# Distance attention: the square root as a power on GpSimd, the clip as a rectified sum on ScalarE; the shared expert in two places

## The reference

```python
scores = jax.nn.sigmoid(xf @ gate_w + bias)
top_scores, top_idx = jax.lax.top_k(scores, K)
top_scores = top_scores / (jnp.sum(top_scores, axis=-1, keepdims=True) + 1e-06)
...
combined = jnp.einsum('teh,te->th', eo * 0.1, w)
shared = (jax.nn.gelu(xf @ sw_up + sb_up, approximate=False) @ sw_down + sb_down) * 0.1
out = (shared + combined).reshape(b, s, h)
out = out / (jnp.max(jnp.abs(out), axis=-1, keepdims=True) + 1e-06)
```

```python
p = jax.nn.softmax(s_, axis=-1) * maskb.astype(scores.dtype)
cum = jnp.cumsum(p, axis=-1)
tot = jnp.sum(p, axis=-1, keepdims=True)
...
dist_scores = jnp.sqrt(jnp.clip((tot - cum) * pos, 0.0, None))
gamma = -jax.nn.softplus(gammas)[None]
diff = jnp.exp(jax.nn.sigmoid(pdiff))[:, None]
total_effect = jnp.clip(jnp.exp(dist_scores * gamma * diff), 1e-05, 100000.0)
scores = scores * total_effect
scores = jax.nn.softmax(scores, axis=-1)
```

## Time and profile before

| | us |
|---|---|
| median of 2 runs | 3798.94 (3797.53 to 3800.35) |
| profiled execution | 3777.61 |
| its span | 3775.8 |

### The profile page before, as it was taken

The page is one execution under the profiler, slowest core; times in us unless marked ns, Lnnn a source line. Parts: engine busy times, 40 slices in busy tenths (PEclk is TensorE's granted clock), DMA queues, the critical chain, the costliest instruction groups (busy, mean ns, idle before and its releaser), DMA issues. The chain is left out here.

```text
span 3775.8 us, 52084 instructions
## 1 busy us (share of the span) xinstructions
PE 3035.1 (80%) x15676; PEld 1663.4 (44%) x15676; DVE 2050.2 (54%) x5067; ACT 1638.2 (43%) x2348; POOL 901.5 (24%) x1035
## 2 busy tenths in 40 slices
PE   5899759687899999875669978899556777777777
PEld 3333459423344444562332245799532434333443
DVE  6677511595333333350478841011367888888853
ACT  1466311120233333220127742233136998898963
POOL 2000010351000000000010003000335777777750
PEclk8899879899999999888879988999877999999998
DMA  4111246341333243349422131599541000000002
GB/s 144 43 47 47 74 163 255 126 167 62 89 71 98 63 105 79 105 181 426 179 72 60 56 125 45 213 345 345 194 146 20 15 17 22 17 22 17 23 9 59
DMA packets 234477, 410.19 MB, mean 109 GB/s; under 512 B 33264, under 2 KB 197872, under 8 KB 210672
## 3 DMA queue, kind: packets, MB, share of 16 engines
q1 hardware_dynamic: 229744, 396.03, 31.7%
q0 software_dynamic: 4608, 12.59, 1.1%
HBM read 325.56 MB, written 82.84 MB: 108 GB/s over the span
## 5 line engine op out<-in xcount | busy, mean ns | idle before, releaser
L2743 DVE TENSOR_TENSOR_SCAN L3x_fade<-L3x_first_exp,L3x_scores 128x513 f32<-128x513 f32 x256 | 311.6, 1217 | 46.8 <-PE L3x_probs_tp L2553 45.9
L2624 POOL TENSOR_TENSOR L3x_fade<-L3x_fade,L3x_apart 128x1024 f32<-128x1024 f32 x128 | 278.8, 2178 | 196.4 <-DVE L3x_mx L2761 157.0
L2550 PE MATMUL L3x_probs_tp<-identity,L3x_fade 128*128 128x128 f32 x1024 | 163.1, 282 | 175.8 <-ACT L3x_probs_T L2689 142.8
L614 DVE TENSOR_REDUCE L1x_neg_max<-L1x_s 128x1 f32<-128x512 f32 x256 | 165.2, 686 | 157.0 <-PE L1x_s L494 156.8
L539 PE MATMUL L1x_o_acc<-L1x_probs_T,L1x_v_unit 128*65 128x512 f32 x512 | 240.1, 592 | 0.0
L2550 PEld LDWEIGHTS L3x_probs_tp<-identity,L3x_fade 128*128 128x128 f32 x1024 | 113.7, 142 | 281.5 <-issue 140.5
L523 PE MATMUL L1x_s<-L1x_q_stack,L1x_k_stack 128*128 128x512 bf16 x768 | 208.3, 380 | 0.0
L699 ACT ACTIVATE L1x_probs_T<-L1x_s 128x1024 f32<-128x1024 f32 x128 | 130.9, 1023 | 161.9 <-PE L1x_s L525 161.9
L2661 ACT ACTIVATE L3x_first_exp<-L3x_scores,L3x_nm 128x512 f32<-128x512 f32 x256 | 175.3, 685 | 53.4 <-DVE L3x_nm L2735 51.7
L930 DVE CUSTOM_DVE_ANT_0 L0x_masked_scores<-L0x_s,L0x_mask_q 128x512 f32<-128x512 f32 x256 | 167.0, 685 | 57.6 <-issue 57.4
L1467 ACT ACTIVATE L2f_hiddenT<-L2f_hidden_ps,L2f_b1s 128x128 f32<-128x128 f32 x320 | 99.9, 363 | 222.8 <-PE L2f_hidden_ps L1402 222.8
(11 more groups left out here) (521 smaller groups left out, 6491.2 us busy)
## 6 DMA issues: line engine op xcount, KB each, us to landing
L2f_w1s<-in_L_w SPq DMA_DIRECT2D x40, 1024.0 KB, 7.5
L2f_w2s<-in_L_w SPq DMA_DIRECT2D x40, 1024.0 KB, 6.4
L1f_w1s<-in_L_w SPq DMA_DIRECT2D x32, 1024.0 KB, 15.5
L1f_w2s<-in_L_w SPq DMA_DIRECT2D x32, 1024.0 KB, 10.6
L1x_q_stack<-L1x_q_parts SPq DMA_DIRECT2D x96, 256.0 KB, 5.3
L0f_w1s<-in_L_w SPq DMA_DIRECT2D x16, 1024.0 KB, 6.1
L0f_w2s<-in_L_w SPq DMA_DIRECT2D x16, 1024.0 KB, 5.2
L1x_k_stack<-L1x_k_parts SPq DMA_DIRECT2D x64, 256.0 KB, 7.4
```

The costliest lines, as they stand in the source:

```text
L2550: nc.tensor.matmul(tp[:, kt, :], fz[:, f, kt * P:(kt + 1) * P], c.ident[:], start=(kt == 0), stop=False, is_transpose=True)
L2624: nc.gpsimd.tensor_tensor(fz[:, f:f + 2, 0:S], fz[:, f:f + 2, 0:S], w, ALU.mult).then_inc(y_done, 1)
L2743: nc.vector.tensor_tensor_scan(fz[:, f, :], ex[:, t, :], sA[:, t, 0:1].to_broadcast([P, S + 1]), 0.0, ALU.add, ALU.bypass).then_inc(f_done, 1)
```

## The change

**In the distance attention** the root is no longer taken by ACT. POOL multiplies as before, waits for that multiplication, and raises the result to the power 0.5 with a second two-operand instruction over the same 2 x 512 columns, the exponent being a broadcast tile. The factor `rl`, which stood under the root, is now a scale: ACT computes the root of `rl` for the four tiles as an exponent of half a logarithm (4 columns), DVE multiplies it by gamma (`gammas`, 4 columns). ACT then computes max(0, scale x z + 11.51) for each tile (`above_floor`) and the exponent of that minus 11.51 (`effect`), which is the factor clipped at 1e-5. Both clips, on DVE and on POOL, are gone. Zeros under the power are replaced by 1e-18, in `ex` and in the table of distances.

**In the top-2 layer** router and shared expert are one block. The logits are computed turned: eight products with 512 tokens as moving columns instead of 32 with 8, then copied and turned back by four transposes. The router's transfers are asked for in the layer norm's block. PE computes half of the shared expert's first batch while DVE works on the router; then ranks, and the rest up to down(1). down(2), up(3) and down(3) stand in the gathering's block, where DVE's additions of tiles 8 to 15 stand inside the gathering loop. The work itself is the same.

```diff
-            shared_expert(c, tag, y, shared, shared_loaded, put_tokens)
...
+                    for k in range(KD):
+                        for b in range(B):
+                            last = nc.tensor.matmul(lgT_ps[32 * b:32 * b + E, :], gate[:, k, :],
+                                                    c.xnT[:, k, b * S:(b + 1) * S], start=(k == 0),
+                                                    stop=(k == KD - 1))
+                    last.then_inc(lgT_done, 1)
+                    pe.wait_ge(lgT_copied, 1)
+                    for i in range(TB):
+                        last = nc.tensor.transpose(lgT_ps[:, i * P:(i + 1) * P], lgT[:, i * P:(i + 1) * P],
+                                                   c.ident[:])
+                    last.then_inc(lg_done, 1)
+                    pe.wait_ge(shared.loaded, 64)
+                    shared.up(pe, hps, 0, range(0, 4))
+                    ranks()
+                    shared.up(pe, hps, 0, range(4, FT))
+                    shared.up(pe, hps, 1, range(FT))
+                    shared.down(pe, ops, 0)
+                    shared.up(pe, hps, 2, range(FT))
+                    shared.down(pe, ops, 1)
...
+                @block.tensor
+                def _(pe):
+                    shared.down(pe, ops, 2)
+                    shared.up(pe, hps, 3, range(FT))
+                    shared.down(pe, ops, 3)
...
                     for t in range(NT + 2):
+                        if 2 * TB <= t < NT:
+                            shared.collect(dve, ops, t)
                         if t < NT:
                             dve.wait_ge(fetched[t % 4], 32 * (t // 4 + 1))
+                            dve.wait_ge(shared.added, t + 1)
...
-                def clip(u, i):
-                    f = (i % 4) * TB + 2
-                    nc.gpsimd.tensor_scalar(fz[:, f:f + 2, 0:S], fz[:, f:f + 2, 0:S], 1e-5, None, ALU.max
-                                            ).then_inc(clip2_done, 1)
...
                     nc.gpsimd.tensor_tensor(fz[:, f:f + 2, 0:S], fz[:, f:f + 2, 0:S], w, ALU.mult).then_inc(y_done, 1)
+                    pool.wait_ge(y_done, u * 2 + (half + 1))
+                    nc.gpsimd.tensor_tensor(fz[:, f:f + 2, 0:S], fz[:, f:f + 2, 0:S],
+                                            power[:].unsqueeze(2).to_broadcast([P, 2, S]), ALU.pow).then_inc(z_done, 1)
...
-                def log(u, i, half):
...
-                        nc.scalar.activation(fz[:, f, 0:S], fz[:, f, 0:S], ACT.Ln, bias=tiny[:], scale=rl[:, f:f + 1]
-                                             ).then_inc(ln_done, 1)
...
-                    nc.scalar.activation(fz[:, f:f + TB, 0:S], fz[:, f:f + TB, 0:S], ACT.Exp, scale=0.5
-                                         ).then_inc(z_done, 1)
+                def root_of_share(u, i):
+                    f = (i % 4) * TB
+                    act.wait_ge(rl_done, u * 2 + 2)
+                    nc.scalar.activation(lrl[:, f:f + TB], rl[:, f:f + TB], ACT.Ln).then_inc(lrl_done, 1)
+                    act.wait_ge(lrl_done, u + 1)
+                    nc.scalar.activation(srl[:, f:f + TB], lrl[:, f:f + TB], ACT.Exp, scale=0.5).then_inc(srl_done, 1)
+
+                def above_floor(u, i, half):
+
+                    act.wait_ge(z_done, u * 2 + (half + 1))
+                    act.wait_ge(gs_done, u + 1)
                     for f in range((i % 4) * TB + 2 * half, (i % 4) * TB + 2 * half + 2):
+                        nc.scalar.activation(fz[:, f, 0:S], fz[:, f, 0:S], ACT.Relu, bias=floor[:, 0:1],
+                                             scale=gs[:, f:f + 1]).then_inc(relu_done, 1)
...
-                                         scale=gamma[:, ds(u % H, 1)]).then_inc(eff_done, 1)
+                    act.wait_ge(relu_done, u * TB + TB)
+                    nc.scalar.activation(fz[:, f:f + TB, 0:S], fz[:, f:f + TB, 0:S], ACT.Exp, bias=floor[:, 1:2]
+                                         ).then_inc(eff_done, 1)
...
-                def clip(u, i):
+                def gammas(u, i):
                     f = (i % 4) * TB
-                    dve.wait_ge(eff_done, u + 1)
-                    nc.vector.tensor_scalar(fz[:, f:f + 2, 0:S], fz[:, f:f + 2, 0:S], 1e-5, None, ALU.max
-                                            ).then_inc(clip_done, 1)
+                    dve.wait_ge(srl_done, u + 1)
+                    nc.vector.tensor_scalar(gs[:, f:f + TB], srl[:, f:f + TB], gamma[:, ds(u % H, 1)], None, ALU.mult
+                                            ).then_inc(gs_done, 1)
```

408 lines of the change are left out of this document (202 added, 206 removed).

## The result

The changed kernel takes 24304.67 us in the median (24301.74 to 24307.59, two runs) against 3798.94, a ratio of 6.402 (95% interval 6.386 to 6.417): 20,506 us more. The prediction was 3707, with a range from 3660 to 4300. One instruction holds the difference.

The account below looks back on a forecast made before the run. Barrier-closed stages; in the attention ACT and DVE are nearly full, then POOL sets the pace (unit 12.25 to 11.4 us). 3798.9 less 38 (top-2 layer) is 3761, less 54 (attention) 3707 us; range 3660 to 4300.

Parts of the forecast that it names:

- What bounds the kernel, and the form of the sum: Attention: no engine full at 12.25 us a unit; then POOL sets the pace at 6.98 + 2s, s one power's price.
- I take the multiplication's price after a wait: Attention, POOL: a power costs 2.08 plus 0.1 us for the wait, s = 2.2; unit 11.4 us, gain 54 us.
- From above: three passes at the clip's price are 8.3 us: Attention, POOL: upper limit on a power's price, built from a logarithm, a product and an exponent.
- The rule of the Trainium skill: POOL's elementwise work: with three or more operations an element, roughly three operations a cycle; two inputs about 2.6 cycles an element.
- Rival 1: Attention, POOL: power in several passes; 3876 us from s = 3.5, 4488 at 8.4; chance 0.17 to s = 6.9, 0.15 beyond.
- The queue behind it: I charge nothing: Attention, POOL: maxima parts stand behind the power, tiles 2 and 3 growing from 2.8 to 5.0 us; charged nothing.
- rival 3: Attention: a stall through tiles 2 and 3 takes the room, 12.1 us a unit, 3751 us; 0.25 shared with two other rivals.
- DVE's product of 4 columns: Attention, DVE: the new product takes about 0.1 us a unit, or some over 1 if POOL holds the shared port.
- ScalarE's terms: Attention, ACT: root gone (1.8 us), rectified sums charged 812 ns like the logarithms, small additions 0.5; about 9.7 us a unit.
- Top-2 layer, 38 us: Top-2 layer: net gain 57.6 - 19.6 = 38 us (30 to 50), giving 3761 us with the layer alone.
- The layer's early block, 57.6 us: Top-2 layer: shared expert's last early addition at 2336 instead of 2393.6, with ranks at 2272.4; gain 57.6 us.
- The layer's late part, 19.6 us: Top-2 layer, gathering: moved shared-expert parts end the stage at 2765.6 instead of 2746.0, a loss of 19.6 us.

Follow-up runs that it names:

- e_mult: The changed kernel with POOL's 128 powers replaced by multiplications by 0.5 (square root left out): 3764.78 us, ratio 0.991.
- e_mult_parts: e_mult with GpSimd's maxima parts issued ahead of its two long instructions: 3728.48 us, ratio 0.982.
- e_mult_gact: e_mult with DVE's product of 4 columns made on ScalarE instead: 3769.76 us, ratio 0.993.
- experiment 7: Runs on the shared expert's late second addition, mostly on the kernel before with the layer's change alone; pausing the scatter after 14 of 32 gave 3736.57 us, 0.985.
- e_split22_timed: Kernel before with the layer's change alone, scatter paused after 22 of 32 until four additions are made: 3729.74 us, ratio 0.986.
- e_layer_only: The kernel before with the top-2 layer's change alone, attention as it was: 3752.74 us, ratio 0.988.
- e_ports: Kernel before, with GpSimd powers and scatters beside small DVE instructions put ahead of its first layer; power over two rows of 512 held SBUF scaling; kernel time not given.
- e_prices: Kernel before, with a list of single GpSimd instructions ahead of its first layer: a power of 1024 columns took 163.2 us; kernel time not given.

## Why the prediction was wrong, step by step

- **What bounds the kernel, and the form of the sum**: right. The unit is 6.98 + 2s; with s = 163.3 that is 333.6 us, measured 333.3. From 3761 us, 63 x (333.3 - 12.25) leads to 23,987; the missing 318 us are the first unit, whose exponent waits for two powers (3169.8, against 2849.8 in the layer-only kernel: 320).
- **"I take the multiplication's price after a wait"**: the step that failed. The term s was 2.2 and measured 163.3, 74 times as much; 128 x 161 us are the 20.6 ms of the miss.
- **"From above: three passes at the clip's price are 8.3 us"**: this bound failed too, by a factor of 20, and with it the range. It wasn't a bound: it assumed that a power is built from three operations that run at the pace of one GpSimd pass. The rows of before had no instruction that bears on this, and then a range can't end there. What the trace did show was that s is unknown, and that each 0.1 us costs 12.6 us. The bound from below, "a lower price than the multiplication's 2.0 is excluded", had no ground either: a product with a broadcast operand takes 1.89 us (e_mult).
- **The rule of the Trainium skill** (GPSIMD Engine Reference, section 3.1) was the right warning and the wrong size: with ten cycles a column it gave an estimate of 8.5 us. Measured: 0.159 us a column, by the page's 1.2 GHz some 191 cycles, an estimate. Either the rule doesn't hold for the power or its thirty operations were far too few; no run here separates the two.
- **Rival 1** is what happened, but even its upper end, 8.4 us, is a nineteenth of the price. The chance of "slower" was 0.32, that of a time beyond 4300 was 0.15.
- **"The queue behind it: I charge nothing"**: wrong, shown by e_mult and e_mult_parts. With an instruction of 1.89 us in the power's place the kernel was 12 us slower than with the layer alone instead of 54 faster, and 36 came back when the parts went ahead. This was rival 3, which gave 3751; e_mult took 3765. I had let GpSimd's own sum cover the ring; but in e_mult GpSimd waits 114 us for DVE's maxima, and each 4.1 us of columns that stand ahead of the parts lengthen the way from maxima to transposes.
- **DVE's product of 4 columns, "0.1 us, or some of them over 1"**: 0.88 us in the mean in e_mult, 161 in the changed kernel. The Trainium skill (SBUF — State Buffer, Who interferes with whom) says that the second waits for the whole other instruction; for this product the trace agrees at 161.0 us. It doesn't for the product of 8 columns with two operands in SBUF, held only to the power's middle (78.0 us), nor for the scaling beside rows of 256 and 128 and the product beside rows of 128, which weren't held at all: there the measurement decides. Taking the product away gained nothing (e_mult_gact).
- **ScalarE's terms**: right. The rectified sums took 804 ns (charged 812), and in e_mult ScalarE is busy 581 of 740 us, so 12.35 x 0.786 = 9.7 us a unit, as worked out.
- **Top-2 layer, 38 us**: the prediction saw that the profiled execution was 21 us under the median and set its differences off from the median all the same. The layer was then timed at the upper level, which differs just here (experiment 7). That the total comes close, 45 us measured for the layer alone (0.988, interval 0.987 to 0.990, so 38 to 51), is in part luck. By traces of one level the layer takes 461.1 us (e_split22_timed) against 509.8 at the lower, 49 less, and 484.6 (e_layer_only) against 526.4 and 529.1 at the upper, 42 to 45 less.
- **The layer's early block, 57.6 us**: 44.2 in the changed kernel's trace, with the second addition late. With all additions on time it is 69, counted from the layer's first instruction to the block's last addition (87.6 us in e_split22_timed, 156.4 before). It is more than forecast because the logits' product took less than the 7 to 14 us: the first copy out of PSUM stood at 2251.41, 2 us behind the first product (2249.44), and the ranks' products at 2263.31 instead of 2272.4.
- **The layer's late part, 19.6 us**: right at the level of the trace that it was read from. From the first gather to the layer's last row the changed kernel takes 66.4 - 46.1 = 20.3 us more (2654.75 to 2721.13, against 2699.56 to 2745.61), and 66.5 - 46.1 = 20.4 in e_split22_timed. At the upper level the kernel before takes 52.0 and 50.9 us there, and the late part costs 14 to 16.

## To carry to other kernels

An operation that no trace shows has no upper bound from its neighbours: on GpSimd two instructions of one shape and one instruction name, a product and a power, differ by 75 times. Run it once alone before it goes into a loop, and if that isn't possible, let the range be open at the top. And in a loop in which no engine is full, cost a change by what stands ahead of the short instruction that another engine waits for, not by the busy sum of its engine. And where the profiled execution and the median of the runs differ, find the stage that holds the difference before you subtract from the one and add to the other.

## What the runs showed of the hardware

- GpSimd's power costs 0.159 us a column whatever the exponent, the base, the second operand and the number of partitions (4, 64 or 128): 1.0 us for 4 columns, 41.1 for 256, 81.9 for 512, 163.2 for 1024.
- A GpSimd power over two rows of 512 columns holds DVE's scaling of 4 columns from SBUF to SBUF until its end (161.0 us), and a product of 8 columns with two SBUF operands until its middle (78.0 us). Over two rows of 256 it didn't hold the scaling (0.78 us for four), over two rows of 128 none of six small forms (0.16 to 0.20 us each).
- GpSimd's multiplication by a broadcast column takes 1.89 us for 1024 columns, by a full operand 2.17.
- Beside GpSimd's indirect transfers DVE's additions, and in e_ports and e_prices TensorE's records too, come late in some comparisons and not in others: the kernel before then takes 3796 to 3800 us instead of 3779 to 3781, and its top-2 layer 526 to 529 us instead of 510. The late addition starts 5.6 to 6.1 us after the last scatter was issued. The cause is open.
